# The last expert layer of an eight-stage kernel: parts of 16, 8 and 8 tiles, and the routing of the last two chunks moved ahead of the units

## What is computed

```python
logits = x @ Wg.T                                  # 4096 tokens, 8 experts
top_v, top_i = jax.lax.top_k(logits, 2)
gates = jax.nn.softmax(top_v, axis=-1)
pos = jnp.cumsum(onehot, axis=0) - 1               # place of each choice in its expert's queue
keep = pos_f < cap                                 # cap = 1280
exp_batches = zeros.at[flat_e, pos_safe].set(x[tok], mode='drop')
h = jnp.einsum('ecd,edf->ecf', exp_batches, W1)    # 128 -> 2 x 256
inp, gate = jnp.split(h, 2, axis=-1)
h = jax.nn.gelu(inp, approximate=False) * gate
exp_out = jnp.einsum('eci,eid->ecd', h, W2)        # 256 -> 128
out = x + sum over the two choices of gate * exp_out[expert, pos], where kept
```

## Time and profile before

| | |
|---|---|
| median of 3 runs | 1501.15 us (1497.45 to 1501.94) |
| profiled execution | 1496.79 us |
| its span, first to last instruction | 1495.0 us |
| mean granted TensorE clock | 0.894 of 2.4 GHz |
| TensorE busy | 1182.6 us (79%) |
| VectorE busy | 990.6 us (66%) |
| ScalarE busy | 671.8 us (45%) |
| GpSimd busy | 536.3 us (36%) |

### The profile page before, as it was taken

The page is one execution under the profiler, slowest core; times in us unless marked ns, Lnnn a source line. Parts: engine busy times, 40 slices in busy tenths (PEclk is TensorE's granted clock), DMA queues, the critical chain, the costliest instruction groups (busy, mean ns, idle before and its releaser), DMA issues. The chain is left out here.

```text
span 1495.0 us, 34936 instructions
## 1 busy us (share of the span) xinstructions
PE 1182.6 (79%) x11141; PEld 925.1 (62%) x11154; DVE 990.6 (66%) x2920; ACT 671.8 (45%) x1427; POOL 536.3 (36%) x590
## 2 busy tenths in 40 slices
PE   2799994349899957779986889999799764898970
PEld 1577773338799925556673466677577654787960
DVE  3689985554533347998974679987677688575342
ACT  1367771115455503445564546676233351443430
POOL 2323303673305257534501233340211125565155
PEclk9999996559999966999998979999799896799995
DMA  6887743012223258535532277553200141233332
GB/s 179 210 207 192 190 104 127 29 55 64 77 75 110 79 130 197 132 99 150 139 82 50 62 175 170 150 147 86 85 0 0 43 139 46 88 119 118 110 112 75
DMA packets 138978, 164.58 MB, mean 110 GB/s; under 512 B 15308, under 2 KB 118754, under 8 KB 131728
## 3 DMA queue, kind: packets, MB, share of 16 engines
q1 hardware_dynamic: 130664, 146.62, 36.6%
q0 software_dynamic: 8192, 16.46, 4.0%
HBM read 111.98 MB, written 51.38 MB: 109 GB/s over the span
## 5 line engine op out<-in xcount | busy, mean ns | idle before, releaser
L586 DVE TENSOR_REDUCE A_neg_max<-A_s_bank 128x4 f32<-128x512 f32 x384 | 253.3, 687 | 48.5 <-PE A_s_bank L725 38.4
L448 ACT ACTIVATE A_probsT<-A_st_bank 128x512 f32<-128x512 f32 x384 | 222.1, 602 | 45.2 <-PE A_st_bank L738 44.2
L725 PE MATMUL A_s_bank<-A_k_stack,A_q_stack 72*128 72x128 bf16 x1536 | 158.9, 229 | 37.6 <-DVE A_neg_max L586 19.0
L738 PE MATMUL A_st_bank<-A_q_stack,A_k_stack 128*128 128x128 bf16 x1536 | 153.2, 224 | 6.9 <-DVE A_q_stack L602 6.2
L738 PEld LDWEIGHTS A_st_bank<-A_q_stack,A_k_stack 128*128 128x128 bf16 x1536 | 113.0, 104 | 52.6 <-issue 42.2
L725 PEld LDWEIGHTS A_s_bank<-A_k_stack,A_q_stack 72*128 72x128 bf16 x1536 | 107.1, 102 | 52.1 <-DVE A_neg_max L586 29.3
L752 PE MATMUL A_pv_bank<-A_probsT,A_v_pad 128*32 128x128 f32 x3072 | 126.7, 283 | 1.0 <-issue 1.0
L2043 ACT ACTIVATE E_h<-E_h_bank,w_L_b 128x256 f32<-128x256 f32 x184 | 76.8, 471 | 82.9 <-PE E_h_bank L2143 81.6
L2143 PE MATMUL E_h_bank<-E_xT,E_w_u 128*128 128x256 f32 x368 | 90.9, 392 | 6.1 <-issue 6.1
L2155 PE MATMUL E_y_bank<-E_w,E_h 128*128 x736 | 91.3, 278 | 2.2 <-ACT E_h L2043 0.9
L2155 PEld LDWEIGHTS E_y_bank<-E_w,E_h 128*128 128x128 f32 x736 | 87.1, 194 | 3.3 <-issue 3.2
(11 more groups left out here) (372 smaller groups left out, 2618.9 us busy)
## 6 DMA issues: line engine op xcount, KB each, us to landing
A_q_stack<-q_scratch SPq DMA_DIRECT2D x48, 576.0 KB
A_k_stack<-k_scratch SPq DMA_DIRECT2D x32, 576.0 KB
q_scratch<-A_q_parts SPq DMA_DIRECT2D x48, 192.0 KB
A_k_stack<-k_scratch SPq DMA_DIRECT2D x48, 192.0 KB
E_xe<-slots_in SPq DMA_DIRECT2D x53, 128.0 KB, 2.1
slots_out<-E_ye SPq DMA_DIRECT2D x53, 128.0 KB, 1.8
A_ctxT<-in_ctxT SPq DMA_DIRECT2D x24, 256.0 KB, 9.9
k_scratch<-A_k_parts SPq DMA_DIRECT2D x32, 192.0 KB
```

Source lines behind the costliest of these rows:

```text
L448: act.activation(probsT[n % 2][:, c * HQ:(c + 1) * HQ, :], st_bank[c % 2][:, :].rearrange("k (a q) -> k a q", a=HQ), ACT.Exp, scale=scale) ...
L586: dve.tensor_reduce(neg_max[:, c * HQ:(c + 1) * HQ], s_bank[c % 2][:, :].rearrange("q (a k) -> q a k", a=HQ), AX.X, ALU.max, negate=True). ...
L725: last = pe.matmul(s_bank[c % 2][:, a * S:(a + 1) * S], q_stack[slot][0:COMBO, h, at:at + S], k_stack[slot][0:COMBO, h, at:at + S], start= ...
L738: last = pe.matmul(dst, k_stack[slot][:, h, at:at + S], q_stack[slot][:, h, at:at + S], start=True, stop=spread)
```

## The change

- `CAPACITY_PARTS` becomes `[(0, 2), (2, 3), (3, 4)]`: 16, 8 and 8 tiles, so 23, 15 and 15 units; still 53.
- Scatters wait for earlier ones from chunk 2 on, no longer from chunk 1 on.
- `table(p)` is cut into three pieces. `table(0)` is no longer in the front stage (a wait for the front's own last addition stands there), but behind `normalise(2)`. The pieces of parts 1 and 2 stand beside units 2, 4, 6 and 8, 10, 12.
- `choose` and `locate` of chunks 2 and 3 stand ahead of the loop over units, `exponent` and `count` of these chunks too; `weigh(2)` and `weigh(3)` beside units 0 and 1; `out_rows` beside 14, 16, 18 and 20 (before 10, 12, 14 and 18).
- First weights have three buffers (`WBUF = 3`) and are copied three units ahead.
- Additions: part 0 from unit 26, part 1 from unit 45, one tile every 5/4 units.

```diff
-CAPACITY_PARTS = [(0, 1), (1, 3), (3, 4)]
+CAPACITY_PARTS = [(0, 2), (2, 3), (3, 4)]
...
-    ADDS = {0: 21, 1: 40}
+    ADDS = {0: 26, 1: 45}
+    WBUF = 3
...
-            return min(ADDS[p] + (b - PARTS[p][0] * RT) * 7 // 8, last_unit) if p in ADDS else last_unit
+            return min(ADDS[p] + (b - PARTS[p][0] * RT) * 5 // 4, last_unit) if p in ADDS else last_unit
...
-                    if c >= 1 and sent[p] and b % PACE == 0:
+                    if c >= 2 and sent[p] and b % PACE == 0:
...
-            def table(p):
+            def table(p, pieces=(0, 1, 2)):
...
+                if 0 in pieces:
+                    for i, c in enumerate((first, last)):
...
+                if 1 in pieces:
+                    own.link(dve.tensor_tensor(hit, per_u(ends[:, :]), per_e(numbers), ALU.is_le))
...
+                if 2 in pieces:
+                    own.link(dve.tensor_tensor(hit, per_u(core.iota8[:, :]), per_e(which[:, 0:n]), ALU.is_equal))
...
+                    dve.sem_inc(table_done, 1)
...
-                if u >= 2:
-                    dve.wait_ge(v_ready, u - 1)
-                dve.tensor_copy(w1_u[u % 2][:, :], w1[:, bass.ds(e * (2 * FC * 128), 2 * FC * 128)]).then_inc(w1_copied, 1)
+                if u >= WBUF:
+                    dve.wait_ge(v_ready, u - WBUF + 1)
+                dve.tensor_copy(w1_u[u % WBUF][:, :], w1[:, bass.ds(e * (2 * FC * 128), 2 * FC * 128)]).then_inc(w1_copied, 1)
...
                 if (g, half) == (6, 1):
-                    table(0)
+                    dve.wait_ge(layer.x_added, START + g + 1)
...
             statistics(3)
             locate(1)
             normalise(2)
+            table(0)
+            normalise(3)
             dve.wait_ge(w1_loaded, 16 * NE)
-            copy_w1(0)
-            copy_w1(1)
-            normalise(3)
+            for u in range(WBUF):
+                copy_w1(u)
             weigh(0)
             weigh(1)
+            choose(2)
+            choose(3)
+            locate(2)
+            locate(3)
             for u in range(last_unit):
-                if u + 2 < last_unit:
-                    copy_w1(u + 2)
+                if u + WBUF < last_unit:
+                    copy_w1(u + WBUF)
                 gate_values(u)
                 if u in (0, 1):
-                    choose(2 + u)
-                if u in (3, 4):
-                    locate(u - 1)
-                if u in (6, 7):
-                    weigh(u - 4)
-                if u in (8, 16):
-                    table(u // 8)
-                if u in (10, 12, 14, 18):
-                    out_rows((10, 12, 14, 18).index(u))
+                    weigh(2 + u)
+                for p in range(1, len(PARTS)):
+                    if u in (6 * p - 4, 6 * p - 2, 6 * p):
+                        table(p, ((u - 6 * p + 4) // 2,))
+                if u in (14, 16, 18, 20):
+                    out_rows((14, 16, 18, 20).index(u))
...
-            exponent(1)
+            for c in range(1, NR):
+                exponent(c)
...
-                if u in (1, 2):
-                    exponent(1 + u)
...
                 logits(2 * c + 1)
+            count(2)
+            count(3)
...
-                if u == 2:
-                    count(2)
-                    count(3)
```

More of the change, by code:

```diff
@@ L2503, in table @@
                 hit = passed[:, 0:n, :]
[L2504 to L2534, removed]
@@ L2535, in table @@
-                dve.sem_inc(table_done, 1)
+                if 0 in pieces:
+                    for i, c in enumerate((first, last)):
+                        own.did(dve.tensor_scalar(kept[:, i, :], base[:, c, :], float(capacity), None, ALU.min))
+                    own.wait()
+                    own.link(dve.tensor_tensor(held[:, :], kept[:, 1, :], kept[:, 0, :], ALU.subtract))
+                    own.did(dve.tensor_scalar(lim[:, :], held[:, :], -float(UT), 0.0, ALU.add, ALU.max))
+                    own.link(dve.tensor_tensor(square[:, :, :], held[:, :, None].to_broadcast([S, NE, MOST]),
+                                               steps[:, None, :].to_broadcast([S, NE, MOST]), ALU.is_gt))
+                    own.link(dve.tensor_reduce(units[:, :], square[:, :, :], AX.X, ALU.add))
+                    own.link(dve.tensor_tensor(square[:, :, 0:NE], upto[:, :, :],
+                                               units[:, None, :].to_broadcast([S, NE, NE]), ALU.mult))
+                    own.link(dve.tensor_reduce(ends[:, :], square[:, :, 0:NE], AX.X, ALU.add))
@@ new lines, in table @@
+                if 1 in pieces:
+                    own.link(dve.tensor_tensor(hit, per_u(ends[:, :]), per_e(numbers), ALU.is_le))
+                    own.link(dve.tensor_reduce(which[:, 0:n], hit[:, :, 0:NE - 1], AX.X, ALU.add))
+                    own.link(dve.tensor_tensor(hit, hit, per_u(ends[:, :]), ALU.mult))
+                    own.link(dve.tensor_reduce(begun[:, 0:n], hit[:, :, 0:NE - 1], AX.X, ALU.max))
+                    own.did(dve.tensor_copy(expert_of[:, at:at + n], which[:, 0:n]))
+                    own.did(dve.tensor_tensor(begun[:, 0:n], numbers, begun[:, 0:n], ALU.subtract))
@@ new lines, in table @@
+                if 2 in pieces:
+                    own.link(dve.tensor_tensor(hit, per_u(core.iota8[:, :]), per_e(which[:, 0:n]), ALU.is_equal))
+                    own.link(dve.tensor_tensor(hit, hit, per_u(lim[:, :]), ALU.mult))
+                    own.link(dve.tensor_reduce(row[:, 0:n], hit, AX.X, ALU.add))
+                    own.did(dve.tensor_scalar(which[:, 0:n], which[:, 0:n], float((last - first) * CT),
+                                              float(first * NE * CT), ALU.mult, ALU.add))
+                    own.link(dve.scalar_tensor_tensor(row[:, 0:n], begun[:, 0:n], float(UT), row[:, 0:n], ALU.mult, ALU.min))
+                    own.link(dve.tensor_tensor(row[:, 0:n], row[:, 0:n], which[:, 0:n], ALU.add))
+                    own.link(dve.tensor_copy(row_of[:, at:at + n], row[:, 0:n]))
+                    own.did(dve.scalar_tensor_tensor(terms[:, p, 2, :], units[:, :], float(UT), lim[:, :], ALU.mult, ALU.subtract))
+                    own.did(dve.tensor_tensor(terms[:, p, 1, :], lim[:, :], begins[:, p, :], ALU.add))
+                    own.link(dve.tensor_tensor(terms[:, p, 0, :], ends[:, :], units[:, :], ALU.subtract))
+                    own.did(dve.tensor_scalar(terms[:, p, 2, :], terms[:, p, 2, :], -float(UT), None, ALU.add))
+                    own.link(dve.scalar_tensor_tensor(terms[:, p, 0, :], terms[:, p, 0, :], float(UT), begins[:, p, :],
+                                                      ALU.mult, ALU.subtract))
+                    dve.sem_inc(table_done, 1)
```

4 lines of the change are left out of this document (2 added, 2 removed).

## The result

The changed kernel takes 1486.33 us, median of 7 runs (1482.31 to 1491.69), against 1501.15 for the kernel before; the ratio is 0.9903, with a 95% interval of 0.9875 to 0.9931. Timed once more beside other kernels it gave 0.9893 (0.9865 to 0.9921). Both intervals lie clear of 1, so the kernel is faster, by some 1.0%; 0.7% was forecast.

The account below looks back on a forecast made before the run. The units on TensorE, with 25.1 us lost to waits, were taken to set when the final 16 gathers begin. +14.0 for the late start and -25.1 for waits gave 11.1 us less, 1501.15 to 1490 us; range 1484 to 1502.

Parts of the forecast that it names:

- Who sets the end: End of the layer: the last unit's store on TensorE's chain, not GpSimd's queue, releases the last 16 gathers; 1453.9 against 1449.
- The late start, +14.0: Start of the units: first load waits for 32 scatters, not 16, so the first unit's result matmuls come 14.0 us later.
- The price of the pace: Scatters of chunk 1 on GpSimd: dropping their three waits of 2.0 us was to save 6 us.
- The cover under the burst: Before the first unit: table, choices and locates moved ahead finish on VectorE at about 1294, with 4 us to spare.
- Choices, locates, exponents: 5.7: First nine unit steps: moving this routing of chunks 2 and 3 out of the units was to gain 5.7 us.
- The tables: 3.2, 2.7 and the clock's 1.6: Tables of parts 1 and 2: cutting into thirds removes TensorE waits of 3.2 and 2.71 us and a clock fall of 1.6.
- The third buffer: 0: Copies of first weights, one unit earlier: worth 0, at most 0.4 us at the start.
- The additions: 9.5 and part of 6.7: Beside later units: asking for tiles slower than gathers deliver removes 9.5 us of waits in part 1, some of 6.7 in part 0.
- The cold start: Rival at the first units: TensorE's clock needs 16 us again after its rest, costing 4.7 us, 1495; chance 0.12.
- The held additions: Rival beside the units: additions still make TensorE wait, at worst keeping part 1's 9.5 us, 1499.5; chance 0.12.
- the choked burst: Rival on GpSimd: 32 unpaced scatters finish only every 3.3 us, 32 us late, 1522; chance 0.06.
- The late burst: Rival before the units: chunk 1's scatters start 2.2 us later or take 1.22 us each, 1492 to 1494; chance 0.08.

## Why the prediction was right, point by point

- *Who sets the end.* Right for the changed kernel: R(52) + 4.1 us, then the last gathers. The two kernels with the pace and with the rate undone move the end by what they move R(52), to 0.1 us.
- *The late start, +14.0.* 13.7 measured. The first load was forecast to 0.1 us. The index of chunk 1 was written at 1269.95, GpSimd ended chunk 0 at 1270.68, so GpSimd was the limit, by 0.6 us, as said; the burst took 19.56 us from first to last start, against 19.5. The price of the pace, "3 x 2.0 = 6", was mis-sized: 5.3, since a wait replaces a gap of 0.30.
- *The cover under the burst.* It held. The last locate ends at T0 + 48.7 (49.1 forecast), the first product starts at T0 + 55.3. GpSimd waited 2.3 us for the index of chunk 2, which held nothing up.
- *Choices, locates, exponents: 5.7.* 5.1 by putting them back.
- *The tables: 3.2, 2.7 and the clock's 1.6.* 7.3 by making them whole again; the thirds cost nothing, as taken.
- *The third buffer: 0.* 0.
- *The additions: 9.5 and part of 6.7.* As a term of the sum in the new split it is right: 10.1 by putting the old rate back. As a reading of the kernel before it isn't: there GpSimd's paced gathers ended at the same time, so that the same cure alone gives 2.3 and not 11. The prediction saw the coincidence at 1465 and computed both paths for the new split, but it booked the wait as the changed rate's gain. It is the gain of the rate and the split together.
- *What was missed.* 2.8 us. R(0) to R(52) is 146.5 and not 147.7, since the last two units have no turn or hidden ahead of them (steps of 2.6 and 1.7 us); R(0) was 0.3 earlier. And the stretch from the last part's first gather to the end, which the prediction took over as 30.0 us that "the change doesn't touch", is 28.7 us. It is 28.7 or 28.8 in all ten profiles of kernels with parts of 16, 8, 8, and 29.9 or 30.0 in all four with 8, 16, 8. The gathers and additions in it take the same time; the difference lies behind them. There the span doesn't end with the last addition and its store: SyncE is through 4.5 us before the block's last semaphores in before and 3.1 us after, and the last to end ahead of those semaphores is a DRAIN on GpSimd's queue (the kernel before, then the changed one; its length in ns three times over, then its start in us):

```profile
L2228 POOLq DRAIN  x1: 21897/21897/21897, 1472.0 to 1472.0; - x1
```

```profile
L2229 POOLq DRAIN  x1: 20267/20267/20267, 1463.2 to 1463.2; - x1
```

  It ends 8.9 us behind the start of the last gather in all ten profiles with 16, 8, 8, and 10.2 us in all four with 8, 16, 8, and the span 1.1 us later in all fourteen. That is the whole 1.3 us. So the forecast was off here because a stretch was copied whole from the kernel before; why GpSimd takes longer to drain with the other split stays open.
- *The rivals.* The cold start: the half clock does cost something, 1.9 us by the kernel with 26 transposes, but that is in the 6.0 us that were copied from before; the clock was back 4 us behind hidden(0), as assumed, and didn't need 16 us again. The held additions and the choked burst didn't come; the latter was priced with 3.3 us for the landing of one scatter, and the median in the burst is 2.2. The late burst was nearer than its chance of 0.08 says: the index was 0.6 us ahead of GpSimd, and in the profile with two buffers a front that was 1.3 us later used this up and made the first load 1 us later.

The change of 11.1 was forecast from one profile against a median difference of 14.8 us. Of the gap of 3.7, 2.8 us is what was missed, above; the rest is within the scatter of the runs.

## What to carry to other kernels

A wait that is removed is worth its length only down to the next queue that ends at the same time; compute both for the new order, and book the gain to the pair. Work that must be done once (routing, tables) belongs under a wait that exists anyway, or in pieces smaller than the slack of one step, and never beside two steps in a row. If a consumer asks at a rate that the supply can't keep, its engine stalls for everybody behind it; asking later costs nothing, and a kernel with a pace is worth a test without it: with parts of 8, 16 and 8 the pace of the gathers protected nothing and cost 10 us.

## What the runs showed of the hardware

TensorE's clock didn't fall behind every rest. A rest of 2.58 us ended with the clock at 1.2 GHz and one of 2.77 us in the same execution at 2.4 GHz; in the kernel before 2.71 us fell and 3.21 us didn't. With 18 extra transposes it fell although the rests ahead of the fall were of 1.2 and 0.7 us. So on a kernel like this one the cost of a rest can be told only to within some 1.6 us.

In all ten profiles with this burst the scatter on GpSimd that falls beside the copies of first weights on VectorE is longer than its neighbours. In the changed kernel it is the scatter beside the three copies (1.20 us from 1280.21), and its neighbour; then the same scatter in the second profile of the same kernel:

```profile
1280.74 1.19 POOL L2402 DMA_INDIRECT slots_in<-E_xn,E_index  x1 [0.30 <-issue]
1282.23 0.97 POOL L2402 DMA_INDIRECT slots_in<-E_xn,E_index  x1 [0.30 <-issue]
```

```profile
1278.55 1.53 POOL L2402 DMA_INDIRECT slots_in<-E_xn,E_index  x1 [0.30 <-issue]
```

That is 0.22 us for all three copies in one execution and 0.56 in the other. Of the ten profiles three have 1.19 us, five 1.53, and the two in which the copies fall otherwise 1.41 and 1.33. So a single profile doesn't give this price, and all of them stay under the 0.75 that the prediction took for three meetings and far under its bound of 4.0. That a hold-up of GpSimd's own DMAs by such a copy is to be expected is what the Trainium skill states ("SBUF — State Buffer", section "SBUF: two separate sides"), and the traces agree with it in kind. No other scatter of the 16 is above 1.10 us in the changed kernel, beside the table, the normalisation and the choices.

Without a pace neither scatters nor gathers grew longer as they followed one another. The 32 scatters of part 0 in the changed kernel go at 1.28 us from one to the next, except around the reciprocal roots (1.4 to 3.2) and beside the copies (1.5); the 32 gathers of part 1 in the kernel with 8, 16 and 8 tiles go at 1.25, with single ones up to 1.37.
